# Mamba look-ahead of a fused Mamba, MoE and feed-forward layer reordered, and the start and end of its feed-forward part

## The reference, cut to what matters

```
x: [4, 1024, 256]                            # 4096 tokens of width 256
h = rmsnorm(x, norm_mamba_w)
z, xBC, dt = split(h @ in_proj_w.T)          # 512, 640, 8 columns
xBC = silu(causal_conv4(xBC) + conv_b);  xs, B, C = split(xBC)   # 512, 64, 64
dt = softplus(dt + dt_bias)                  # one value per token and head, 8 heads
state = state * exp(dt * A) + dt * xs (x) B;  y = state . C      # scan over 1024 tokens
h = rmsnorm((y + D*xs) * silu(z)) @ out_proj_w.T + x
x1 = layernorm(x + h + moe(rmsnorm(h)))      # 8 experts, 2 for each token, 1024 wide
g = silu((x1 @ w_gate) * s_gate) * ((x1 @ w_up) * s_up)          # 1024 wide
out = layernorm(x1 + (g @ w_down) * s_down)
```

## Time and profile before

| | |
|---|---|
| median of 3 runs | 1174.09 us (1173.02 to 1177.39) |
| the profiled execution's own time | 1173.58 us |
| its span, first to last instruction | 1172.0 us |
| mean granted TensorE clock | 0.988 |
| PE busy | 1106.3 us, 94% |
| DVE busy | 684.1 us, 58% |
| ACT busy | 618.1 us, 53% |
| POOL busy | 372.8 us, 32% |

### The profile page before, as it was taken

The page is one execution under the profiler, slowest core; times in us unless marked ns, Lnnn a source line. Parts: engine busy times, 40 slices in busy tenths (PEclk is TensorE's granted clock), DMA queues, the critical chain, the costliest instruction groups (busy, mean ns, idle before and its releaser), DMA issues.

```text
span 1172.0 us, 21801 instructions
## 1 busy us (share of the span) xinstructions
PE 1106.3 (94%) x7492; PEld 983.4 (84%) x7493; DVE 684.1 (58%) x1651; ACT 618.1 (53%) x1276; POOL 372.8 (32%) x331
## 2 busy tenths in 40 slices
PE   4799999999999999889999999999999999999995
PEld 3587878787878786789999999999999997888885
DVE  4686767676777776677332332323233257889875
ACT  4665655555656564254454545445454555556653
POOL 1323134334343435347404030404040225445101
PEclk9999999999999999889999999999999999999998
DMA  3030102020201011238231313313131223213101
GB/s 119 1 112 4 39 1 77 1 73 6 69 10 63 15 46 53 88 119 278 88 115 36 117 45 116 116 45 106 49 114 45 81 70 115 69 59 113 46 19 54
DMA packets 40340, 81.70 MB, mean 70 GB/s; under 512 B 5840, under 2 KB 30032, under 8 KB 38992
## 3 DMA queue, kind: packets, MB, share of 16 engines
q1 hardware_dynamic: 22768, 35.47, 9.1%
q0 software_dynamic: 7440, 35.66, 8.9%
q10 hardware_dynamic: 10064, 9.70, 2.4%
HBM read 48.05 MB, written 31.72 MB: 68 GB/s over the span
## 4 chain that ended last, share of the span: by engine, by line
PE 66%; DVE 13%; issue 9%; ACT 7%; POOL 2%; SPq 1%; DMA 1%; DVEq 0%; ACTq 0%; POOLq 0%
PE e_bank L1161 6%; PE e_bank L1178 6%; PE e_bank L1180 6%; PE e_bank L1179 6%; PE e_bank L1162 6%; PE e_bank L1163 6%; PE f_bank L1300 4%; PE f_bank L1299 4%; PE bank L1042 3%; DVE decay L1479 2%; PE bank L1068 2%; PE f_bank L1312 2%; PE f_bank L1313 2%; PE bank L957 2%; PE bank L1111 2%
## 5 line engine op out<-in xcount | busy, mean ns | idle before, releaser
L1565 DVE TENSOR_TENSOR e_h_lo<-e_bank,e_h_hi 128x512 fp32r<-128x512 f32 x148 | 102.1, 691 | 283.3 <-ACT e_bank L761 283.0
L1161 PE MATMUL e_bank<-e_x_hi,e_w_hi 128*128 128x256 f32 x592 | 169.7, 287 | 1.4 <-issue 1.3
L1178 PE MATMUL e_bank<-e_w_hi,e_h_hi 128*128 128x256 f32 x592 | 170.5, 288 | 0.5 <-DVE e_h_lo L1565 0.5
L1163 PE MATMUL e_bank<-e_x_hi,e_w_lo 128*128 128x256 f32 x592 | 168.4, 285 | 0.0
L1162 PE MATMUL e_bank<-e_x_lo,e_w_hi 128*128 128x256 f32 x592 | 168.4, 284 | 0.0
L1180 PE MATMUL e_bank<-e_w_hi,e_h_lo 128*128 128x256 f32 x592 | 167.6, 283 | 0.0
L1179 PE MATMUL e_bank<-e_w_lo,e_h_hi 128*128 128x256 f32 x592 | 167.5, 283 | 0.0
L759 ACT ACTIVATE e_h_hi<-e_bank 128x512 fp32r<-128x512 f32 x148 | 88.4, 598 | 77.1 <-PE e_bank L1163 73.0
L1429 DVE SCALAR_TENSOR_TENSOR conv<-raw,conv_w,conv 128x512 f32<-128x512 f32 x120 | 95.3, 795 | 42.2 <-ACT conv L679 39.4
L1161 PEld LDWEIGHTS e_bank<-e_x_hi,e_w_hi 128*128 128x128 f32 x592 | 114.6, 194 | 3.0 <-issue 3.0
L1162 PEld LDWEIGHTS e_bank<-e_x_lo,e_w_hi 128*128 128x128 f32 x592 | 114.6, 194 | 0.0
(11 more groups left out here) (249 smaller groups left out, 2689.4 us busy)
## 6 DMA issues: line engine op xcount, KB each, us to landing
e_stage<-in_w POOLq DMA_DIRECT2D x9, 2048.0 KB, 8.0
e_x_rows<-sent_rows SPq DMA_DIRECT2D x37, 256.0 KB
back_rows<-e_y_rows ACTq DMA_DIRECT2D x37, 256.0 KB, 2.2
x_in<-in_x SPq DMA_DIRECT2D x8, 512.0 KB, 4.4
x_res_dram<-x_res SPq DMA_DIRECT2D x8, 512.0 KB, 2.9
f_res<-x_res_dram SPq DMA_DIRECT2D x8, 512.0 KB, 3.8
out<-f_out_t SPq DMA_DIRECT2D x8, 512.0 KB, 2.6
back_rows<-zeros SPq DMA_DIRECT2D x12, 256.0 KB, 3.3
```

Source lines behind the costliest of these rows:

```text
L1161: mm(out, w1h[:, k, t], x_hi[:, k], start=k == 0, stop=False)
L1163: r = mm(out, w1l[:, k, t], x_hi[:, k], start=False, stop=k == KD - 1)
L1178: mm(out, eh_hi[:, k, t], w2h[:, k], start=k == 0, stop=False)
L1565: tt(flat(eh_lo[:, 2 * p:2 * p + 2]), h_ps[p][:], flat(eh_hi[:, 2 * p:2 * p + 2]).bitcast(F32), ALU.subtract).then_inc(es["h_lo_ready"], 1)
```

## The change

1. The `dt` products (`dt_proj`), `softplus_in` and `softplus` move from w = 1 and 2 into w = 0, `softplus_out` to the start of w = 1. ACT's `softplus` no longer loads a table: in w = 0 the exp table is still in. `convolve` and `conv_out` of tiles 1 to 3 take other places.
2. `la` gets two buffers, and POOL spreads one chunk in each iteration (w = 1, 2, 3, 0) in place of two in w = 3 and two in w = 0. Where `it` is at most 0, a spread still waits for nothing of the scan.
3. `xm` gets three buffers. The second half of a group's sends moves from w = 2 to the end of w = 3.
4. FF's start: both gathers of groups 0 and 1 ahead of the first power; the mix of group 1 ahead of the first `fuse`; its statistics, scale and transposes one or two units sooner; the third gather in one piece, behind both powers.
5. FF's end: the last group is finished in three pieces (chunks 0 and 1, chunk 2, chunk 3). The down product of its last chunk goes to a bank of its own.

The `seg` products themselves are not changed. The diff, without the edits that only add an index of a buffer or the names of semaphores:

```diff
-LA_T, DECAYS, CONVS, X_INS = 2, 6, 3, 3
+LA_T, DECAYS, CONVS, X_INS, XMS = 2, 6, 3, 3, 3
...
-            for g in range(NG):
+            for g in range(NG - 1):
                 f_store(g)
+            for j, (c, end) in enumerate(PIECES):
+                sp.wait_ge(fs["end_out"], j + 1)
+                sp.dma_start(out[NG - 1][:, c:end], f_out[:, 1, c:end]).then_inc(fs["out_stored1"], 16)
             sp.wait_ge(fs["out_stored0"], 16 * (NG // 2))
-            sp.wait_ge(fs["out_stored1"], 16 * (NG // 2))
+            sp.wait_ge(fs["out_stored1"], 16 * (NG // 2 - 1 + len(PIECES)))
...
+                if ahead and w:
+                    spread(g, w - 1, it)
+                if w == 0 and 0 <= g - 1 < NG:
+                    spread(g - 1, 3, it)
                 if w == 2:
                     if 0 <= g + 1 < NG:
                         norm(g + 1)
                     if 0 <= g - 3:
                         send(g - 3, (0, 1))
-                if ahead and w == 3:
-                    spread(g, 0, it)
-                    spread(g, 1, it)
-                if w == 0 and 0 <= g - 1 < NG:
-                    spread(g - 1, 2, it)
-                    spread(g - 1, 3, it)
                 if 0 <= it < NQ:
                     y_norm(it)
-                if w == 2 and 0 <= g - 3:
+                if w == 3 and 0 <= g - 3 < NG - 2:
                     send(g - 3, (2, 3))
...
-            f_deviation(0, f_norm, "var_ready", "x1_ready", "rs_ready")
             pool.wait_ge(es["y_stored"], 16 * (need[1] + 1))
             nc.gpsimd.tensor_tensor(f_seen[:, 1:2], half[:, 0:1], half[:, 1:2], ALU.subtract)
             f_gather(1)
+            f_deviation(0, f_norm, "var_ready", "x1_ready", "rs_ready")
+            f_deviation(1, f_norm, "var_ready", "x1_ready", "rs_ready")
             pool.wait_ge(es["y_stored"], 16 * (ended + LAST + 1))
             nc.gpsimd.tensor_tensor(f_seen[:, 2:3], half[:, 0:1], half[:, 1:2], ALU.subtract)
-            f_gather(2, range(CH))
-            f_deviation(1, f_norm, "var_ready", "x1_ready", "rs_ready")
-            f_gather(2, range(CH, 2 * CH))
-            for g in range(NG + 2):
+            f_gather(2)
+            for g in range(NG + 1):
                 if 1 <= g and g + 1 < NG:
                     f_deviation(g + 1, f_norm, "var_ready", "x1_ready", "rs_ready")
                 if g >= 2:
                     f_deviation(g - 2, f_norm2, "var2_ready", "out_ready", "rs2_ready")
                 if g + 3 < NG:
                     f_gather(g + 3)
+            pool.wait_ge(fs["out_ready"], NG - 1)
+            for j, (c, end) in enumerate(PIECES):
+                pool.wait_ge(fs["end_var"], j + 1)
+                nc.gpsimd.tensor_tensor(f_norm2[:, 1, c:end], f_norm2[:, 0, c:end], half[:, c:end], ALU.pow)\
+                    .then_inc(fs["end_rs"], 1)
...
             def softplus(g):
                 act.wait_ge(s["soft_in"], g + 1)
-                nc.scalar.preload_act_table_set("natural_log_exp_and_others")
                 nc.scalar.activation(soft[:, 2], soft[:, 1], ACT.Exp).then_inc(s["soft_exp"], 1)
                 act.wait_ge(s["soft_exp"], 2 * g + 1)
...
-                if c == 0:
-                    wait(act, s[f"xm_sent{g % 2}"], 16 * 2 * CH * (g // 2))
-                nc.scalar.activation(xm[:, g % 2, c, :], h1[:, q % 2], ACT.Copy, scale=tail_stat[:, q % 2, 5:6])\
+                if c == 0 and g >= XMS:
+                    act.wait_ge(s[f"xm_sent{(g - XMS) % 2}"], 16 * 2 * CH * ((g - XMS) // 2 + 1))
+                nc.scalar.activation(xm[:, g % XMS, c, :], h1[:, q % 2], ACT.Copy, scale=tail_stat[:, q % 2, 5:6])\
                     .then_inc(s["xm_ready"], 1)
...
                 if ahead and w == 2:
-                    conv_out(g, 2)
-                    softplus(g)
+                    conv_out(g, 1)
                 if w == 2 and 0 <= g + 1 < NG and g + 1 != 1:
                     squares(g + 1)
                 if ahead and w == 2:
-                    conv_out(g, 3)
+                    conv_out(g, 2)
                     tap(g, 4)
                 if ahead and w == 3:
+                    conv_out(g, 3)
                     conv_out(g, 4)
                     nc.scalar.preload_act_table_set("natural_log_exp_and_others")
                 if scan:
                     y_squares(it)
-                if ahead and w == 1:
-                    conv_out(g, 1)
...
                 if w == 0:
                     if ahead:
+                        softplus(g)
                         raw_out(g, 1)
...
-                if f == (3 if g else 5) and g + 1 < NG:
+                if f == 3 and g + 1 < NG:
...
-            f_scale2(NG - 1)
+            act.wait_ge(fs["out_stored1"], 16 * (NG // 2 - 1))
+            for j, (c, end) in enumerate(PIECES):
+                act.wait_ge(fs["end_shift"], j + 1)
+                for n in range(c, end):
+                    i = nc.scalar.activation(f_out[:, 1, n], f_y[:, 1, n], ACT.Identity, bias=f_norm2[:, 2, n:n + 1],
+                                             scale=f_norm2[:, 1, n:n + 1])
+                i.then_inc(fs["end_out"], 1)
...
-                    wait(pe, s["yg_ready"], CH * g - 3)
+                    wait(pe, s["yg_ready"], CH * g - 4)
+                    wait(pe, s["pex_ready"], g)
...
-                wait(pe, s["soft_in"], min((q + 7) // CH, NG))
+                wait(pe, s["soft_in"], min((q + 8) // CH, NG))
...
                 if w == 0:
                     if ahead:
                         tile(g, 0)
+                        dt_proj(g, 0)
+                        dt_proj(g, 1)
                     if 0 <= g - 1 < NG:
                         seg(g - 1, 2)
+                    if ahead:
+                        dt_proj(g, 2)
+                        dt_proj(g, 3)
                 if ahead and w == 1:
                     tile(g, 2)
-                    dt_proj(g, 0)
                     tile(g, 3)
-                    dt_proj(g, 1)
...
                 if ahead and w == 1:
-                    dt_proj(g, 2)
                     tile(g, 4)
-                    dt_proj(g, 3)
...
+                if g == NG - 1 and c == CH - 1:
+                    o = fxt_ps[0][:, 0:D]
...
-                    if f == (4 if g else 6) and g + 1 < NG:
+                    if f == (4 if g else 5) and g + 1 < NG:
...
-                wait(dve, s["seg_done"], 2 * CH * g)
-                ts(la[:].rearrange("p c h -> p (c h)"), m, DECAY_MIN, None, ALU.max).then_inc(s["la_ready"], 1)
+                wait(dve, s["seg_done"], 2 * CH * (g - 1))
+                ts(flat(la[:, g % 2]), m, DECAY_MIN, None, ALU.max).then_inc(s["la_ready"], 1)
...
                 if ahead and w == 1:
-                    convolve(g, 1)
+                    softplus_out(g)
                 if w == 2:
                     if ahead:
-                        softplus_in(g)
-                        convolve(g, 3)
+                        convolve(g, 2)
...
                 if ahead and w == 0:
+                    softplus_in(g)
                     if g % 2:
                         halo(g)
                     convolve(g, 0)
                 if ahead and w == 1:
-                    convolve(g, 2)
+                    convolve(g, 1)
                 if scan and it % SEQ != SEQ - 1:
                     hand_on(it)
                 if ahead and w == 2:
-                    softplus_out(g)
+                    convolve(g, 3)
...
                     if f == 0:
-                        mix_first(1)
+                        f_stats(1, 0, f_mixed[:, 1], "mixed_both", "mix_stats")
                     if f == 1:
-                        mix_second(1)
+                        mix_moments(1)
                     if f == 2:
-                        f_stats(1, 0, f_mixed[:, 1], "mixed_both", "mix_stats")
-                    if f == 3:
-                        mix_moments(1)
-                    if f == 4:
                         mix_shift(1)
...
+            mix_first(1)
+            mix_second(1)
             for n in range(NG * KF):
                 fuse(n)
                 if n:
                     f_part(n - 1)
                 between(*divmod(n, KF))
             f_part(NG * KF - 1)
-            for g in (NG, NG + 1):
-                for f in range(KF):
-                    between(g, f)
+
+            def end_stats(j):
+                c, end = PIECES[j]
+                dve.wait_ge(fs["down_done"], CH * (NG - 1) + end)
+                ps = (down_ps[0][:], down_ps[1][:, 0:D], fxt_ps[0][:, 0:D])[j]
+                tt(f_y[:, 1, c:end], ps.rearrange("p (c d) -> p c d", d=D),
+                   bcast(f_s_down[:], 1, end - c), ALU.mult).then_inc(fs["end_scaled"], 1)
+                dve.wait_ge(fs["end_scaled"], j + 1)
+                tt(f_y[:, 1, c:end], f_y[:, 1, c:end], f_x1[:, (NG - 1) % X1_BUFS, c:end], ALU.add)\
+                    .then_inc(fs["end_added"], 1)
+                dve.wait_ge(fs["end_added"], j + 1)
```

(33 more changed lines are left out.)

22 lines of the change are left out of this document (12 added, 10 removed).

## The result

The changed kernel takes 1170.43 us (median of nine runs, 1163.25 to 1175.30) against 1174.09: a ratio of 0.9960, 95% interval 0.9945 to 0.9976, so less than the 0.5% that counts as a change here. The forecast was 1169.0.

A forecast was written before the change was run, and what follows sets the result against it. PE's own program was taken to set the time, so only its idle time could be won. The terms 6.3 - 1.9 - 1.3 + 0.3 + 1.7 = 5.1 us gave 1169.0, range 1164.5 to 1174.5.

The forecast's parts named there:

- Steady groups: Six steady Mamba groups: shorter z waits win 3.9 us and w = 3 wins 2.4; together 6.3 us, range 0 to 9.
- ACT was held by DVE there, not by its own load: Steady w = 2: DVE's chain moves forward by only 0.65 us, the z wait shrinks from 1.19 to about 0.55.
- w = 3 term: Steady w = 3: with four sends moved POOL is early and PE's 0.37 us wait goes; 2.4 us in six groups.
- Rival (b): Steady groups: what PE wins in w = 2 and 3 it waits for in w = 0 or 1; time 1175.3, chance 0.10.
- (d): Steady w = 0: `raw_out` 1 comes late behind `softplus`, `seg` waits; at 2 us the kernel takes 1183; chance 0.06.
- First group: First Mamba group: spreads beside the second tile's convolution delay z, slow matmuls follow; 1.9 us lost, bounds +1.6 to -3.5.
- the prediction is wrong if the first group's z wait shrinks: Sign set beforehand: PE's z wait in the first group was to grow from 4.04 to 5.4 us.
- Rival (a): The first group and the passage to the experts hide their delays; sum 9.9 us, time 1164.2, chance 0.17.
- Rival (c): Steady w = 2: a spread blocks `x_res` by up to 0.4 us, the z wait keeps it; time 1171.4, chance 0.07.
- Passage: Passage to the experts: later sends delay `rows_in`, PE stands until 512.5; half of 2.5 us counted, 1.3 lost.
- FF's start: FF's first groups: PE gains 1.5 us, gives it back waiting for group 2's power behind sixteen gathers; +0.3 us.
- FF's end: Behind PE's last matmul: finishing in pieces ends ACT at 1165.9, not 1167.43, and shortens the store; 1.7 us won (1 to 3.5).

The follow-up runs named there:

- table_back: The changed kernel, but ACT again loads the other table in w = 2 and silu's table behind it; 1.0053 of the time of the kernel before.
- sends_old: The changed kernel, but the second half of a group's sends is again in w = 2 behind y_norm; 0.9961 of the time of the kernel before.
- first_old: The changed kernel, but group 0 keeps the order of before on every engine; 0.9957 of the time of the kernel before.
- spread_wait: The changed kernel, but group 0's spreads on POOL wait for four convolutions of that group; 0.9932 of the time of the kernel before.
- after_again: The changed kernel run once more with nothing altered, beside the kernel before; ratio 0.9970, at equal clock -5.3 us.

## Why the prediction was right, and where it wasn't

The range and the class held; the mechanism held in part. By the terms:

- **Steady groups, +6.3.** Right in sign, too small: 8.45, in every execution. PE's listed waits between the markers fell from 9.6 to 3.4 us (z 6.4 to 3.1, `y_gated` 1.5 to 0, `decay` 1.7 to 0.3): 6.2, almost the forecast. The other 2.3 us are matmuls that follow each other more closely; why is open. (The 18.74 of 20 us given with the earlier trace rows is the window from 300 to 320; the row shown has 19.47.) The mechanism was half wrong. "ACT was held by DVE there, not by its own load" was read from one group's 0.36 us; `table_back` shows the two loads costing 5.3 us in the new order. The w = 3 term of 2.4 us was counted for six groups; `sends_old` gives about 1.5 in four. Rival (b) is out, and (d): no wait of `seg` for `raw` appeared.
- **First group, -1.9.** Measured -2.46 in the profiles; `first_old` gets back 1.5. The size was near by luck, the step wrong: I put the convolution's 3.1 us on the path and the `dt` products at nothing. In before PE's matmuls of 512 columns started 0.43 us apart until 20.73 and 0.23 apart from 21.09. In after the 24 small products came first (4.98 us in place of 2.4), and the tiles behind them kept the 0.43 us until 32.56 (0.23 from 32.87). So PE ended the first two z tiles at 37.92 in place of 32.95, 5.0 us late; the z wait shrank from 4.04 to 2.05, not above 5, and the third z tile started 3.0 us late. In `spread_wait` the convolution's share is 0.6 us of `z_out`. By my own test, "the prediction is wrong if the first group's z wait shrinks", this step failed. Rival (a) is out too: the first group's delay shows.
- **Rival (c).** In most steady groups the spread and `x_res` overlap by only 0.15 us (307.08 to 308.98, 308.83), and the sum takes 0.43 us as ever. Where they overlap by more, it was blocked. After, then before:

```profile
132.41 1.90 POOL L492 TENSOR_TENSOR la_t<-la,le 128x1024 f32<-128x1024 f32 x1 [3.20 <-issue]
133.76 0.83 DVE L1513 TENSOR_TENSOR x_res<-h,x_in 128x256 f32<-128x256 f32 x1
```
```profile
86.48 3.75 POOL L487 TENSOR_TENSOR la_t<-la,le 128x1024 f32<-128x1024 f32 x2 [2.40 <-DVE y_in L1441]
89.02 1.49 DVE L1498 TENSOR_TENSOR x_res<-h,x_in 128x256 f32<-128x256 f32 x1
```

The sum ended 0.28 us behind the spread both times. So the rival's mechanism was there, in one group of the six, worth the 0.4 us it named for one. `spread_wait`, where this overlap is gone, has 347.17 for the six groups in place of 347.54. The row I held against it, 0.43 us at 327.89, began 0.15 us ahead of the first spread's end, and the second spread took 2.08 us in place of 1.90. The Trainium skill's rule (SBUF — State Buffer, section "Who interferes with whom"), that a DVE instruction with two SBUF inputs contends with a GpSimd one that reads SBUF, agrees with this and with the convolutions: 7.60 us for six beside two spreads, 4.56 without.

- **Passage, -1.3 (0 to -2.5).** `rows_in` was issued 7.18 us behind `y_norm`, as worked out, and landing took 2.7, not 3.3. By the passage table the loss is 1.3 to 2.4. Halving the wait was the mis-sized step: PE's wait for rows was 1.13 at 501.98, near the half counted, but a second one of 1.47 followed at 527.40, where the rows took 10.7 us to land. A third of 2.63 at 542.20 has its like in before (2.70 at 551.81).
- **FF's start, +0.3 (0 to 1.9).** 0.9 in the first profile, the power of group 2 0.9 us sooner; the wait behind it 1.09 us, not above 2. Alone, in another job, the start was 3.5 us slower at equal clock, a loss that I had excluded.
- **FF's end, +1.7.** Measured 0.0. ACT's last instruction came 6 us behind PE's, as forecast. The step that failed is "and 4.6 us of store and end": I hung the end on the store. It hangs on POOL's last instruction. The rows that show it were in the profile of before.

At equal clock the whole change is worth about 5 us: after_again shows 5.3, and the terms 8.45 - 2.5 - 2.1 + 0.9 + 0 give 4.8. The forecast's sum of 5.1 is near that, by errors that cancelled: 2.2 too little in the steady part and 0.6 in FF's start, 1.7 too much at the end and 1.3 in first group and passage together. That the sum came near was luck. The medians' difference of 3.7 us doesn't contradict it: its interval is 2.8 to 6.5 us, and the clock differs between executions by as much as the change is worth.
